# Seven blocks in the first group, deeper steps in the second, three raw slots instead of four

## The chip, the cores and the metric

One core of a Trainium2 chip runs the whole kernel. The metric is the device time of one execution in microseconds (us); the kernel before takes 721.62 us (median of three runs, 721.6 to 721.69). TensorE is called PE here, VectorE DVE, ScalarE ACT, GpSimd POOL and SyncE SP.

## The reference

`x` is 8192 x 128, `adj` is 8192 x 8192, W is 128 x 128, b has 128 values, all float32.

```python
h = maximum(layernorm(x), 0)
out = x + relu(adj @ (h @ W) + b)
```

The kernel computes `(adj @ h) @ W`. `adj` is 268 MB and has to be read once; that and the product adj @ h are nearly all of the work.

## The kernel before

**Tiling.** The 8192 rows of adj, which become output rows, are cut into 16 blocks of 512; the 8192 columns, over which is summed, into 64 k-tiles of 128. The product of one block and one k-tile is a [128 x 128] x [128 x 512] matmul into one of the eight PSUM banks; the tile of h is the weight and the piece of adj (transposed by the host, 256 KB) the moving side. Float32 precision comes from splitting: `high` is adj rounded to fp32r (ACT copies it, L404), `low` is the rest (DVE subtracts, L543), h has both halves too, and every block and k-tile gets three matmuls in a row of kinds: high x h_high, high x h_low, low x h_high (`product`, L582 to L587). The first two k-tiles of the first group (FOUR_PASS) aren't split: PE multiplies plain float32 (L627) while the vector engines are still at the layer norm.

**Groups and steps.** The blocks are worked in four groups of 6, 2, 6 and 2 (WIDTHS). A step t takes `DEPTHS` k-tiles of all blocks of its group: one k-tile in the wide groups, three in the narrow ones, so that every step has six blocks' worth of adj (1.5 MB). There are 64 + 22 + 64 + 22 = 172 steps, numbered through. A step's adj comes in pieces (`split_of`, L71): three pieces of two blocks in steps 2 to 23, two of three blocks in steps 24 to 63, and one piece of six in all later steps but the last. Each piece has its own DMA, and ACT, DVE and PE wait piece by piece (`parts_of`, L94; steps 4 to 9 halve their last piece block by block).

**Buffers.** `raw` has 4 slots (what DMA brings), `high` 3, `low` 2. SP issues the loads of step t once DVE has finished `low` of step t - 4 (L297). ACT writes high of step t after low of step t - 3 and PE's use of high of step t - 3 (L399, L400). DVE writes low of step t after all products of step t - 2 (L539). PE waits for the parts of high and of low (L642, L657).

**Layer norm.** During the first group x is loaded in 17 batches; DVE, ACT and POOL compute mean, variance and the normalised z, and ACT and DVE make h_high and h_low, four k-tiles at a time.

**Draining a group.** While a group runs, the blocks of the one before are drained in other PSUM banks. Step `FIRST_STEP + DRAIN_AT[c]` drains block c (`drained_at`, L160): there ACT copies the sum (L384) and DVE takes the rest (L498); one step later (PROJECT_AFTER) PE multiplies with W in three matmuls (`project`, L605); four steps later (FINISH_AFTER) DVE adds and takes the maximum (`finish`, L502); nine steps later (STORE_AFTER) SP stores. The residual x of the block, 256 KB, is loaded by SP in the draining step itself (`load_residual`, L273), into one of four slots of `x_sb`, after that slot's last store has landed (L278); POOL adds the bias to it (L356). SP does all that in one queue with the loads of adj: a wait for a store or for an output holds up the adj loads behind it. PE starts the third and fourth group only when all blocks of the group before the last are finished (L639). The last two blocks are closed one by one (L691 to L707).

Of the kernel before, what the change touches and what calls it, by code (L numbers as in the profile page):

```python
# [7 lines left out]
BANK = 512  # L8
N = 8192
TILES = N // P  # L10
COL_BLOCKS = N // BANK
# [1 line left out]

WIDTHS = [6, 2, 6, 2]
DEPTHS = [1, 3, 1, 3]
FIRST_BLOCK = [0, 6, 8, 14]
FIRST_BANK = [0, 6, 0, 6]
STEPS = [-(-TILES // d) for d in DEPTHS]  # L20
FIRST_STEP = [sum(STEPS[:g]) for g in range(len(WIDTHS))]
ALL_STEPS = sum(STEPS)
LAST = ALL_STEPS - 1

RAW_SLOTS, HIGH_SLOTS, LOW_SLOTS = 4, 3, 2
WIDEST = max(w * d for w, d in zip(WIDTHS, DEPTHS)) * BANK


# [5 lines left out]

FOUR_PASS = 2

NARROW_UNTIL = 24

HALVED_SINGLY = range(4, 10)

LOW_AT_ONCE_UNTIL = 7
WARMING, WARM = 2, 448
X_SLOTS = 4
Z_SLOTS = 2


DRAIN_AT = [3, 6, 8, 11, 13, 16]
PROJECT_AFTER, FINISH_AFTER, STORE_AFTER = 1, 4, 9
OUT_SLOTS = 2
EPS = 1e-5  # L50

# [19 lines left out]
def split_of(t):  # L71

    g = group_of(t)
    if t == 0:
        return [1, 1, 2, 2]
    if g == 0:
        return [3, 3] if t < FOUR_PASS or t >= NARROW_UNTIL else [2, 2, 2]
    return [1] * WIDTHS[g] if t == LAST else [WIDTHS[g]]


# [79 lines left out]
def drained_at(t, after):  # L160

    for g in range(len(WIDTHS) - 1):
        for c in range(WIDTHS[g]):
            if FIRST_STEP[g + 1] + DRAIN_AT[c] + after == t:
                return FIRST_BLOCK[g] + c
    return None

# [6 lines left out]
def gnn_layer(nc, x_batches, x_blocks, adj_piece, W, b, out_blocks):  # L174
    with ExitStack() as ctx:  # L175
# [36 lines left out]
        raw_landed = [[sem(f"raw_landed{s}_{i}") for i in range(4 if s == 0 else 3)] for s in range(RAW_SLOTS)]  # L212
        x_landed = [sem(f"x_landed{s}") for s in range(X_SLOTS)]
        x_first_landed = sem("x_first_landed")
        res_landed = [sem(f"res_landed{s}") for s in range(X_SLOTS)]
        params_landed = sem("params_landed")
        constants_ready = sem("constants_ready")
        warm_ready = sem("warm_ready")
# [27 lines left out]
        last_sum_ready = sem("last_sum_ready")  # L246
        last_projected = sem("last_projected")
        output_ready = sem("output_ready")
        stored = [sem(f"stored{s}") for s in range(X_SLOTS)]
        block = ctx.enter_context(nc.Block())  # L250

        def columns(t):
            g = group_of(t)
# [5 lines left out]
        @block.sync  # L259
        def _(sp):  # L260
            def load_x(j):

                if j == 5:
                    sp.wait_ge(centred, EARLY)
                if j > 5:
                    sp.wait_ge(z_ready, BATCHES[j - X_SLOTS][1] - EARLY)
                sp.dma_start(x_sb[:, x_slot(j), :], x_batches[j]).then_inc(x_landed[x_slot(j)], 16)  # L267

            def load_piece(t, i):
                sp.dma_start(raw[:, t % RAW_SLOTS, columns_of(t, blocks_of(t, i))], adj_piece(t, i)) \  # L270
                  .then_inc(raw_landed[t % RAW_SLOTS][i], 16)

            def load_residual(n):  # L273
                if n < X_SLOTS:

                    sp.wait_ge(z_ready, TILES - EARLY)
                else:
                    sp.wait_ge(stored[n % X_SLOTS], 16 * (n // X_SLOTS))  # L278
                sp.dma_start(x_sb[:, n % X_SLOTS, :], x_blocks[n]).then_inc(res_landed[n % X_SLOTS], 16)

            def store(n):
                sp.wait_ge(output_ready, n + 1)
                sp.dma_start(out_blocks[n], x_sb[:, n % X_SLOTS, :]).then_inc(stored[n % X_SLOTS], 16)

            sp.dma_start(x_sb[:, 0, 0:P], x_batches[0]).then_inc(x_first_landed, 16)  # L285

            for i in (0, 2, 3):
                load_piece(0, i)
            for t in range(1, ALL_STEPS):
                if t == 2:  # L290
                    load_x(3)
                if RAW_SLOTS <= t < RAW_SLOTS + FOUR_PASS:

                    sp.wait_ge(products_done, t - RAW_SLOTS + 1)
                if t >= RAW_SLOTS + FOUR_PASS:

                    sp.wait_ge(low_ready, halved(t - RAW_SLOTS))  # L297
                for i in range(len(split_of(t))):
                    load_piece(t, i)
                if mean_at(t) is not None:  # L300
                    load_x(mean_at(t))
                if t == 30:
                    sp.dma_start(W_sb[:, :], W).then_inc(params_landed, 16)
                    sp.dma_start(bias[:, :], b).then_inc(params_landed, 16)
                n = drained_at(t, 0)
                if n is not None:
                    load_residual(n)
                n = drained_at(t, STORE_AFTER)
                if n is not None:
                    store(n)  # L310
            for n in range(FIRST_BLOCK[-1], COL_BLOCKS):
                load_residual(n)
            for t in range(ALL_STEPS, ALL_STEPS + STORE_AFTER):
                n = drained_at(t, STORE_AFTER)
                if n is not None:
                    store(n)
            for n in range(FIRST_BLOCK[-1], COL_BLOCKS - 1):
                store(n)
            n = COL_BLOCKS - 1
            sp.wait_ge(output_ready, n + 1)  # L320
            sp.dma_start(out_blocks[n][:, 0:HALF], x_sb[:, n % X_SLOTS, 0:HALF]).then_inc(stored[n % X_SLOTS], 16)
            for s in range(X_SLOTS):

                sp.wait_ge(stored[s], 16 * (COL_BLOCKS // X_SLOTS + (s == n % X_SLOTS)))

        @block.gpsimd
        def _(pool):
            nc.gpsimd.memset(minus_half[:, :], -0.5).then_inc(constants_ready, 1)
            pool.wait_ge(constants_ready, 1)
            for j, (first, end) in enumerate(BATCHES):  # L330
                pool.wait_ge(var_ready, j + 1)
                nc.gpsimd.tensor_tensor(rstd[:, first:end], var_eps[:, first:end],  # L332
                                        minus_half[:, first:end], ALU.pow).then_inc(rstd_ready, 1)
                if j < 2:
                    continue
                pool.wait_ge(rstd_ready, j + 1)
                if j < SUMMED_BY_DVE:
                    pool.wait_ge(centre_ready, j + 1)

                if j == 3:  # L340
                    pool.wait_ge(h_first_ready, FOUR_PASS)
                    pool.wait_ge(early_low, EARLY - FOUR_PASS)
                if j > 3:
                    pool.wait_ge(h_low_ready, BATCHES[j - Z_SLOTS][1] - EARLY)
                for t in range(first, end):
                    cols = slice(t % 4 * P, t % 4 * P + P)
                    nc.gpsimd.tensor_scalar(z_sb[:, x_slot(j) % Z_SLOTS, cols],  # L347
                                            x_sb[:, x_slot(j), cols],
                                            neg_mean[:, t:t + 1], rstd[:, t:t + 1],
                                            ALU.add, ALU.mult).then_inc(z_ready, 1)  # L350
            pool.wait_ge(params_landed, 32)
            nc.gpsimd.tensor_scalar(neg_bias[:, :], bias[:, :], -1.0, None, ALU.mult).then_inc(neg_bias_ready, 1)
            for n in range(COL_BLOCKS):

                pool.wait_ge(res_landed[n % X_SLOTS], 16 * (n // X_SLOTS + 1))
                nc.gpsimd.tensor_scalar(x_sb[:, n % X_SLOTS, :], x_sb[:, n % X_SLOTS, :], bias[:, 0:1], None,  # L356
                                        ALU.add).then_inc(x_biased, 1)

        @block.scalar
        def _(act):  # L360
# [60 lines left out]
            for half in range(2):  # L421
# [1 line left out]
                nc.scalar.activation(last_sum[:, cols], banks[:, bank_of(n), cols],  # L423
                                     ACT.Copy).then_inc(last_sum_ready, 1)
            act.wait_ge(output_ready, n + 2)
            act.dma_start(out_blocks[n][:, HALF:BANK], x_sb[:, n % X_SLOTS, HALF:BANK]) \
               .then_inc(stored[n % X_SLOTS], 16)

        @block.vector
        def _(dve):  # L430
# [71 lines left out]
            def finish(n):  # L502
                dve.wait_ge(x_biased, n + 1)
                dve.wait_ge(projected, n + 1)
                nc.vector.scalar_tensor_tensor(x_sb[:, n % X_SLOTS, :], banks[:, bank_of(n), :], neg_bias[:, 0:1],  # L505
                                               x_sb[:, n % X_SLOTS, :], ALU.max, ALU.add) \
                  .then_inc(output_ready, 1)

            def finish_last(half):
                n = COL_BLOCKS - 1  # L510
                cols = slice(half * HALF, (half + 1) * HALF)
                dve.wait_ge(last_projected, half + 1)
                nc.vector.scalar_tensor_tensor(x_sb[:, n % X_SLOTS, cols], banks[:, half, 0:HALF],  # L513
                                               neg_bias[:, 0:1], x_sb[:, n % X_SLOTS, cols],
                                               ALU.max, ALU.add).then_inc(output_ready, 1)

            for cols in (slice(0, P), slice(P, WARM)):
# [63 lines left out]
        def _(pe):  # L581
# [49 lines left out]
            for t in range(FOUR_PASS, LAST - 1):  # L631
# [2 lines left out]
                opens, closes = s == 0, s == STEPS[g] - 1  # L634
                depths = range(depth_of(t))
                parts = parts_of(t)
                if opens and g >= 2:

                    pe.wait_ge(output_ready, FIRST_BLOCK[g - 1])  # L639

                def with_high(part):
                    pe.wait_ge(high_ready, halved(t, part))  # L642
                    if part == 0:
                        high_is_there(t)
                    for k in depths:
# [102 lines left out]
```

## Time and profile before

| what | value |
|---|---|
| median of three runs | 721.62 us |
| the profiled execution | 721.9 us |
| its span, first to last instruction | 720.1 us |
| PE busy, matmuls | 715.2 us (99%), 3113 |
| PE weight loads | 583.8 us (81%) |
| DVE busy | 623.3 us (87%) |
| ACT busy | 517.5 us (72%) |
| POOL busy | 181.4 us (25%) |
| DMA | 281.60 MB, mean 391 GB/s |
| granted PE clock | 1.00 throughout |

The profile is of one execution; 1.8 us of it lie outside the span, and it is 0.3 us above the median. Matmuls overlap in the pipeline: one is shown as 390 ns long though a new one starts about every 227 ns. So PE's idle time is read best from the idle time before its weight loads (PEld), which is 0.04 us where nothing is waited for. "Landing" is the time from the issue of a DMA to its completion.

### The profile page before, as it was taken

To read this page: it belongs to the slowest core of one execution; us is meant where nothing else is said; L and a number is where in the kernel's file an instruction comes from. 1 tells how busy PE (TensorE), PEld (TensorE's weight loads), DVE (VectorE), ACT (ScalarE), POOL (GpSimd) and SP (SyncE) were. 2 spreads that over 40 slices of the span, in tenths; PEclk is the share of its full clock that TensorE was granted. 3 is DMA by queue.
4 is the path that set the end of the run, shared out by engine and by line. 5 is a ranking of instruction groups with operands and counts; after the bars stand their busy time and mean duration, and the time that the engine had idled before them with its cause. 6 is when DMAs were issued, how large, how long until landed. Compare 5 with 4: busy or idle time off the path is not lost.

```text
span 720.1 us, 7905 instructions
## 1 busy us (share of the span) xinstructions
PE 715.2 (99%) x3113; PEld 583.8 (81%) x3113; DVE 623.3 (87%) x394; ACT 517.5 (72%) x400; POOL 181.4 (25%) x99
## 2 busy tenths in 40 slices
PE   9999999999999999999999999999999999999998
PEld 4878888888888888888888888888888888888886
DVE  5999999999999888988798888878788887888895
ACT  2788888888888767766577667667676676767662
POOL 4445555556544402410041000000000000033023
PEclk9999999999999999999999999999999999999999
DMA  9999999999999999999999999999999999999992
GB/s 353 408 408 409 409 411 415 412 415 416 417 415 414 418 421 407 415 387 404 359 410 428 383 402 396 364 397 386 379 390 391 382 391 385 398 403 397 389 382 77
DMA packets 45110, 281.60 MB, mean 391 GB/s; under 512 B 5137, under 2 KB 5777, under 8 KB 31505
## 3 DMA queue, kind: packets, MB, share of 16 engines
q1 hardware_dynamic: 44496, 280.25, 97.2%
q10 hardware_dynamic: 576, 0.85, 0.4%
q8 instruction: 24, 0.39, 0.2%
q14 instruction: 14, 0.11, 0.0%
HBM read 276.89 MB, written 4.19 MB: 390 GB/s over the span
## 4 chain that ended last, share of the span: by engine, by line
PE 94%; DMA 3%; DVE 1%; SPq 0%; ACT 0%; issue 0%; DVEq 0%; ACTq 0%
PE banks L585 93%; DMA raw<-adj 3%; DVE low L543 1%; PE banks L612 0%; PE banks L613 0%; PE banks L611 0%; SPq L270 0%; ACT high L404 0%; DVE h_low L489 0%; DVE x_sb L505 0%; DVE x_sb L513 0%; SPq L267 0%; DVEq L175 0%; SPq L285 0%; ACTq L403 0%
## 5 line engine op out<-in xcount | busy, mean ns | idle before, releaser
L543 DVE TENSOR_TENSOR low<-raw,high 128x3072 fp32r<-128x3072 f32 (+3 forms) x261 | 576.5, 2235 | 83.1 <-PE banks L585 69.9
L404 ACT ACTIVATE high<-raw 128x3072 fp32r<-128x3072 f32 (+3 forms) x261 | 483.6, 1864 | 188.6 <-DMA raw<-adj 160.7
L585 PE MATMUL banks<-high,h_high 128*128 128x512 f32 x1012 | 272.7, 390 | 0.1
L585 PE MATMUL banks<-high,h_low 128*128 128x512 f32 x1012 | 272.0, 389 | 0.0
L585 PE MATMUL banks<-low,h_high 128*128 128x512 f32 x1012 | 268.5, 389 | 0.0
L585 PEld LDWEIGHTS banks<-high,h_high 128*128 128x128 f32 x1012 | 189.6, 188 | 41.1 <-ACT high L404 1.6
L585 PEld LDWEIGHTS banks<-low,h_high 128*128 128x128 f32 x1012 | 189.7, 188 | 40.1 <-DVE low L543 0.8
L585 PEld LDWEIGHTS banks<-high,h_low 128*128 128x128 f32 x1012 | 190.0, 188 | 39.5
L356 POOL TENSOR_SCALAR x_sb<-x_sb,bias 128x512 f32<-128x512 f32 x16 | 54.5, 3409 | 414.2 <-DMA x_sb<-x_blocks 414.2
L347 POOL TENSOR_SCALAR z_sb<-x_sb,neg_mean,rstd 128x128 f32<-128x128 f32 x60 | 94.7, 1590 | 1.6
L332 POOL TENSOR_TENSOR rstd<-var_eps,minus_half 128x4 f32<-128x4 f32 (+2 forms) x17 | 31.6, 1860 | 112.8 <-DVE var_eps L447 103.6
L369 ACT ACTIVATE squares<-x_sb,neg_mean 128x128 f32<-128x128 f32 x52 | 20.1, 387 | 0.0
L384 ACT ACTIVATE sum_high<-banks 128x512 fp32r<-128x512 f32 x15 | 8.7, 580 | 7.0 <-PE banks L585 7.0
L505 DVE SCALAR_TENSOR_TENSOR x_sb<-banks,neg_bias,x_sb 128x512 f32<-128x512 f32 x15 | 11.2, 744 | 2.2 <-PE banks L613 2.2
L498 DVE TENSOR_TENSOR sum_low<-banks,sum_high 128x512 fp32r<-128x512 f32 x15 | 10.3, 683 | 2.1 <-ACT sum_high L384 2.1
L627 PE MATMUL banks<-raw,h_first 128*128 128x512 f32 x24 | 11.1, 607 | 0.2
L489 DVE SCALAR_TENSOR_TENSOR h_low<-z_sb,h_high 128x512 fp32r<-128x512 f32 x15 | 10.3, 690 | 0.0
L627 PEld LDWEIGHTS banks<-raw,h_first 128*128 128x128 f32 x24 | 4.2, 189 | 7.5 <-issue 4.5
L369 ACT ACTIVATION_READ_ACCUMULATOR squares<-x_sb,neg_mean 128x1 f32 x52 | 9.8, 188 | 0.0
L376 ACT ACTIVATE h_high<-z_sb 128x512 fp32r<-128x512 f32 x15 | 9.2, 614 | 0.0
L436 DVE TENSOR_REDUCE neg_sum<-x_sb 128x4 f32<-128x512 f32 x13 | 8.8, 674 | 0.0
L458 DVE BATCH_NORM_STATS2 stats<-x_sb 128x6 f32<-128x128 f32 x12 | 2.7, 282 | 4.4 <-DMA x_sb<-x 4.4
(34 smaller groups left out, 47.8 us busy)
## 6 DMA issues: line engine op xcount, KB each, us to landing
raw<-adj SPq DMA_DIRECT2D x106, 1536.0 KB, 8.6
raw<-adj SPq DMA_DIRECT2D x82, 768.0 KB, 10.6
raw<-adj SPq DMA_DIRECT2D x69, 512.0 KB, 11.9
x_sb<-x_blocks SPq DMA_DIRECT2D x16, 256.0 KB, 8.4
out_blocks<-x_sb SPq DMA_DIRECT2D x15, 256.0 KB, 8.7
x_sb<-x SPq DMA_DIRECT2D x14, 256.0 KB, 12.2
raw<-adj SPq DMA_DIRECT2D x3, 256.0 KB, 6.5
raw<-adj ACTq DMA_DIRECT2D x1, 256.0 KB, 2.8
```

The costliest lines, as they stand in the source:

```text
L332: nc.gpsimd.tensor_tensor(rstd[:, first:end], var_eps[:, first:end], minus_half[:, first:end], ALU.pow).then_inc(rstd_ready, 1)
L347: nc.gpsimd.tensor_scalar(z_sb[:, x_slot(j) % Z_SLOTS, cols], x_sb[:, x_slot(j), cols], neg_mean[:, t:t + 1], rstd[:, t:t + 1], ALU.add, A ...
L356: nc.gpsimd.tensor_scalar(x_sb[:, n % X_SLOTS, :], x_sb[:, n % X_SLOTS, :], bias[:, 0:1], None, ALU.add).then_inc(x_biased, 1)
L369: nc.scalar.activation(squares[:, before % 4, :], x_sb[:, x_slot(j), cols], ACT.Square, bias=neg_mean[:, t:t + 1], accum_out=sum_squares[: ...
L376: nc.scalar.activation(h_high[:, first:end, :], z_sb[:, x_slot(j) % Z_SLOTS, :].rearrange("p (t d) -> p t d", d=P), ACT.Relu).then_inc(h_h ...
L404: nc.scalar.activation(high[:, t % HIGH_SLOTS, cols], raw[:, t % RAW_SLOTS, cols], ACT.Copy).then_inc(high_ready, 1)
L489: nc.vector.scalar_tensor_tensor(h_low[:, first:end, :], z_sb[:, x_slot(j) % Z_SLOTS, :] .rearrange("p (t d) -> p t d", d=P), 0.0, h_high[ ...
L498: nc.vector.tensor_tensor(sum_low[:, n % OUT_SLOTS, :], banks[:, bank_of(n), :], sum_high[:, n % OUT_SLOTS, :].bitcast(F32), ALU.subtract) ...
L505: nc.vector.scalar_tensor_tensor(x_sb[:, n % X_SLOTS, :], banks[:, bank_of(n), :], neg_bias[:, 0:1], x_sb[:, n % X_SLOTS, :], ALU.max, ALU ...
L543: nc.vector.tensor_tensor(low[:, t % LOW_SLOTS, cols], raw[:, t % RAW_SLOTS, cols], high[:, t % HIGH_SLOTS, cols].bitcast(F32), ALU.subtra ...
L585: return nc.tensor.matmul(banks[:, FIRST_BANK[g] + c, :], h[:, (t - FIRST_STEP[g]) * DEPTHS[g] + k, :], tile[:, slot, at:at + BANK], start ...
L627: last = nc.tensor.matmul(banks[:, FIRST_BANK[0] + c, :], h_first[:, t, :], raw[:, t, c * BANK:(c + 1) * BANK], start=t == 0, stop=False)
```

## The change

The groups become 7, 1, 6 and 2 blocks wide, and the second takes six k-tiles a step, so it has 11 steps of 1.5 MB (the last of four k-tiles) and all together are 161. The first group's steps have seven blocks (1.75 MB). Buffers of a step are as wide as the widest step, so each slot grows from 6 to 7 blocks, and `raw` goes from 4 slots to 3; high and low keep 3 and 2. Pieces are [1, 1, 2, 3] in step 0, [4, 3] in step 1 and from step 20 to 63, [3, 2, 2] between; the third group's steps come in two pieces of three blocks instead of one of six. Draining: the six blocks of banks 0 to 5 are drained in steps 1, 2, 4, 5, 7 and 8 of the second group; the seventh stays in bank 6 and is drained in step 15 counted from the second group's start, which is step 4 of the third (counted from 0), and the second group's only block in step 8 of the third. The fourth group drains as before. Finishing comes three steps after draining (four before), storing eight (nine before), and the residual is loaded two steps ahead. Residuals have six slots: the four of `x_sb` and the two of `z_sb`. The opening step of the third and fourth group waits part by part for the banks that this part writes.

```diff
--- before.py
+++ after.py
@@ -13,16 +13,16 @@
 
 
 
-WIDTHS = [6, 2, 6, 2]
-DEPTHS = [1, 3, 1, 3]
-FIRST_BLOCK = [0, 6, 8, 14]
-FIRST_BANK = [0, 6, 0, 6]
+WIDTHS = [7, 1, 6, 2]
+DEPTHS = [1, 6, 1, 3]
+FIRST_BLOCK = [0, 7, 8, 14]
+FIRST_BANK = [0, 7, 0, 6]
 STEPS = [-(-TILES // d) for d in DEPTHS]
 FIRST_STEP = [sum(STEPS[:g]) for g in range(len(WIDTHS))]
 ALL_STEPS = sum(STEPS)
 LAST = ALL_STEPS - 1
 
-RAW_SLOTS, HIGH_SLOTS, LOW_SLOTS = 4, 3, 2
+RAW_SLOTS, HIGH_SLOTS, LOW_SLOTS = 3, 3, 2
 WIDEST = max(w * d for w, d in zip(WIDTHS, DEPTHS)) * BANK
 
 
@@ -34,18 +34,20 @@
 
 FOUR_PASS = 2
 
-NARROW_UNTIL = 24
+NARROW_UNTIL = 20
 
 HALVED_SINGLY = range(4, 10)
 
 LOW_AT_ONCE_UNTIL = 7
 WARMING, WARM = 2, 448
 X_SLOTS = 4
+RES_SLOTS = 6
 Z_SLOTS = 2
 
 
-DRAIN_AT = [3, 6, 8, 11, 13, 16]
-PROJECT_AFTER, FINISH_AFTER, STORE_AFTER = 1, 4, 9
+
+DRAIN_AT = [[1, 2, 4, 5, 7, 8, 15], [8], [3, 6, 8, 11, 13, 16]]
+RESIDUAL_AHEAD, PROJECT_AFTER, FINISH_AFTER, STORE_AFTER = 2, 1, 3, 8
 OUT_SLOTS = 2
 EPS = 1e-5
 
@@ -72,9 +74,11 @@
 
     g = group_of(t)
     if t == 0:
-        return [1, 1, 2, 2]
+        return [1, 1, 2, 3]
     if g == 0:
-        return [3, 3] if t < FOUR_PASS or t >= NARROW_UNTIL else [2, 2, 2]
+        return [4, 3] if t < FOUR_PASS or t >= NARROW_UNTIL else [3, 2, 2]
+    if g == 2:
+        return [3, 3]
     return [1] * WIDTHS[g] if t == LAST else [WIDTHS[g]]
 
 
@@ -161,7 +165,7 @@
 
     for g in range(len(WIDTHS) - 1):
         for c in range(WIDTHS[g]):
-            if FIRST_STEP[g + 1] + DRAIN_AT[c] + after == t:
+            if FIRST_STEP[g + 1] + DRAIN_AT[g][c] + after == t:
                 return FIRST_BLOCK[g] + c
     return None
 
@@ -212,7 +216,7 @@
         raw_landed = [[sem(f"raw_landed{s}_{i}") for i in range(4 if s == 0 else 3)] for s in range(RAW_SLOTS)]
         x_landed = [sem(f"x_landed{s}") for s in range(X_SLOTS)]
         x_first_landed = sem("x_first_landed")
-        res_landed = [sem(f"res_landed{s}") for s in range(X_SLOTS)]
+        res_landed = [sem(f"res_landed{s}") for s in range(RES_SLOTS)]
         params_landed = sem("params_landed")
         constants_ready = sem("constants_ready")
         warm_ready = sem("warm_ready")
@@ -246,8 +250,13 @@
         last_sum_ready = sem("last_sum_ready")
         last_projected = sem("last_projected")
         output_ready = sem("output_ready")
-        stored = [sem(f"stored{s}") for s in range(X_SLOTS)]
+        stored = [sem(f"stored{s}") for s in range(RES_SLOTS)]
         block = ctx.enter_context(nc.Block())
+
+        def residual(n):
+
+            slot = n % RES_SLOTS
+            return x_sb[:, slot, :] if slot < X_SLOTS else z_sb[:, slot - X_SLOTS, :]
 
         def columns(t):
             g = group_of(t)
@@ -274,13 +283,16 @@
                 if n < X_SLOTS:
 
                     sp.wait_ge(z_ready, TILES - EARLY)
+                elif n < RES_SLOTS:
+
+                    sp.wait_ge(h_low_ready, TILES - EARLY)
                 else:
-                    sp.wait_ge(stored[n % X_SLOTS], 16 * (n // X_SLOTS))
-                sp.dma_start(x_sb[:, n % X_SLOTS, :], x_blocks[n]).then_inc(res_landed[n % X_SLOTS], 16)
+                    sp.wait_ge(stored[n % RES_SLOTS], 16 * (n // RES_SLOTS))
+                sp.dma_start(residual(n), x_blocks[n]).then_inc(res_landed[n % RES_SLOTS], 16)
 
             def store(n):
                 sp.wait_ge(output_ready, n + 1)
-                sp.dma_start(out_blocks[n], x_sb[:, n % X_SLOTS, :]).then_inc(stored[n % X_SLOTS], 16)
+                sp.dma_start(out_blocks[n], residual(n)).then_inc(stored[n % RES_SLOTS], 16)
 
             sp.dma_start(x_sb[:, 0, 0:P], x_batches[0]).then_inc(x_first_landed, 16)
 
@@ -302,12 +314,12 @@
                 if t == 30:
                     sp.dma_start(W_sb[:, :], W).then_inc(params_landed, 16)
                     sp.dma_start(bias[:, :], b).then_inc(params_landed, 16)
-                n = drained_at(t, 0)
-                if n is not None:
-                    load_residual(n)
                 n = drained_at(t, STORE_AFTER)
                 if n is not None:
                     store(n)
+                n = drained_at(t, -RESIDUAL_AHEAD)
+                if n is not None:
+                    load_residual(n)
             for n in range(FIRST_BLOCK[-1], COL_BLOCKS):
                 load_residual(n)
             for t in range(ALL_STEPS, ALL_STEPS + STORE_AFTER):
@@ -318,10 +330,10 @@
                 store(n)
             n = COL_BLOCKS - 1
             sp.wait_ge(output_ready, n + 1)
-            sp.dma_start(out_blocks[n][:, 0:HALF], x_sb[:, n % X_SLOTS, 0:HALF]).then_inc(stored[n % X_SLOTS], 16)
-            for s in range(X_SLOTS):
-
-                sp.wait_ge(stored[s], 16 * (COL_BLOCKS // X_SLOTS + (s == n % X_SLOTS)))
+            sp.dma_start(out_blocks[n][:, 0:HALF], residual(n)[:, 0:HALF]).then_inc(stored[n % RES_SLOTS], 16)
+            for s in range(RES_SLOTS):
+
+                sp.wait_ge(stored[s], 16 * (len(range(s, COL_BLOCKS, RES_SLOTS)) + (s == n % RES_SLOTS)))
 
         @block.gpsimd
         def _(pool):
@@ -352,8 +364,8 @@
             nc.gpsimd.tensor_scalar(neg_bias[:, :], bias[:, :], -1.0, None, ALU.mult).then_inc(neg_bias_ready, 1)
             for n in range(COL_BLOCKS):
 
-                pool.wait_ge(res_landed[n % X_SLOTS], 16 * (n // X_SLOTS + 1))
-                nc.gpsimd.tensor_scalar(x_sb[:, n % X_SLOTS, :], x_sb[:, n % X_SLOTS, :], bias[:, 0:1], None,
+                pool.wait_ge(res_landed[n % RES_SLOTS], 16 * (n // RES_SLOTS + 1))
+                nc.gpsimd.tensor_scalar(residual(n), residual(n), bias[:, 0:1], None,
                                         ALU.add).then_inc(x_biased, 1)
 
         @block.scalar
@@ -423,8 +435,8 @@
                 nc.scalar.activation(last_sum[:, cols], banks[:, bank_of(n), cols],
                                      ACT.Copy).then_inc(last_sum_ready, 1)
             act.wait_ge(output_ready, n + 2)
-            act.dma_start(out_blocks[n][:, HALF:BANK], x_sb[:, n % X_SLOTS, HALF:BANK]) \
-               .then_inc(stored[n % X_SLOTS], 16)
+            act.dma_start(out_blocks[n][:, HALF:BANK], residual(n)[:, HALF:BANK]) \
+               .then_inc(stored[n % RES_SLOTS], 16)
 
         @block.vector
         def _(dve):
@@ -502,16 +514,16 @@
             def finish(n):
                 dve.wait_ge(x_biased, n + 1)
                 dve.wait_ge(projected, n + 1)
-                nc.vector.scalar_tensor_tensor(x_sb[:, n % X_SLOTS, :], banks[:, bank_of(n), :], neg_bias[:, 0:1],
-                                               x_sb[:, n % X_SLOTS, :], ALU.max, ALU.add) \
+                nc.vector.scalar_tensor_tensor(residual(n), banks[:, bank_of(n), :], neg_bias[:, 0:1],
+                                               residual(n), ALU.max, ALU.add) \
                   .then_inc(output_ready, 1)
 
             def finish_last(half):
                 n = COL_BLOCKS - 1
                 cols = slice(half * HALF, (half + 1) * HALF)
                 dve.wait_ge(last_projected, half + 1)
-                nc.vector.scalar_tensor_tensor(x_sb[:, n % X_SLOTS, cols], banks[:, half, 0:HALF],
-                                               neg_bias[:, 0:1], x_sb[:, n % X_SLOTS, cols],
+                nc.vector.scalar_tensor_tensor(residual(n)[:, cols], banks[:, half, 0:HALF],
+                                               neg_bias[:, 0:1], residual(n)[:, cols],
                                                ALU.max, ALU.add).then_inc(output_ready, 1)
 
             for cols in (slice(0, P), slice(P, WARM)):
@@ -634,12 +646,12 @@
                 opens, closes = s == 0, s == STEPS[g] - 1
                 depths = range(depth_of(t))
                 parts = parts_of(t)
-                if opens and g >= 2:
-
-                    pe.wait_ge(output_ready, FIRST_BLOCK[g - 1])
 
                 def with_high(part):
                     pe.wait_ge(high_ready, halved(t, part))
+                    if opens and g >= 2:
+
+                        pe.wait_ge(output_ready, FIRST_BANK[g] + parts[part][1][-1] + 1)
                     if part == 0:
                         high_is_there(t)
                     for k in depths:
```

## Rows read from the trace of the kernel before

**Rows 1.** The page: busy share, then the granted clock in 40 slices.

```profile
PE 715.2 (99%) x3113; PEld 583.8 (81%) x3113; DVE 623.3 (87%) x394; ACT 517.5 (72%) x400; POOL 181.4 (25%) x99
...
PEclk9999999999999999999999999999999999999999
```

**Rows 2.** Busy time by stretch: PE, PEld, DVE, ACT, POOL, clock, DMA share, GB/s.

```profile
352.00:614.00 262.00, 262.00 (x1157) 216.91 (x1156) 217.91 (x70) 177.63 (x66) 10.60 (x2) 1.00 0.99 392
614.00:705.00 91.00, 91.00 (x402) 75.19 (x401) 78.64 (x33) 62.99 (x30) 21.87 (x7) 1.00 0.98 388
sum 645.00, PE 645.00 PEld 533.71 DVE 566.03 ACT 475.17 POOL 152.19; mean PE 129.00 PEld 106.74 DVE 113.21 ACT 95.03 POOL 30.44
```

**Rows 3.** Waits from 60 to 712 us: us in total, times, longest.

```profile
ACT high L404 <- DMA raw<-adj: 143.4, 142, 3.0
...
DVE low L543 <- PE banks L585: 69.9, 89, 2.9
```

**Rows 4.** Waits in the first 60 us.

```profile
PEld banks L627 <- DMA raw<-adj: 1.7, 2, 1.0
PEld banks L585 <- ACT high L404: 1.6, 5, 0.5
...
PEld banks L585 <- DVE low L543: 0.8, 3, 0.4
```

**Rows 5.** PE's weight loads at the start: start us, us, in brackets idle before.

```profile
8.68 0.30 PEld L627 LDWEIGHTS banks<-raw,h_first 128*128 128x128 f32 x2 [0.95 <-DMA raw<-adj]
9.22 0.19 PEld L627 LDWEIGHTS banks<-raw,h_first 128*128 128x128 f32 x1 [0.24 <-issue]
...
15.34 0.19 PEld L585 LDWEIGHTS banks<-high,h_high 128*128 128x128 f32 x1 [0.29 <-ACT high L404]
...
36.79 0.30 PEld L585 LDWEIGHTS banks<-high,h_high 128*128 128x128 f32 x2 [0.48 <-ACT high L404]
```

**Rows 6.** Busy time by stretch at the start, columns as in rows 2.

```profile
4.00:15.30 11.30, 11.06 (x25) 4.23 (x24) 6.55 (x37) 1.06 (x1) 4.61 (x8) 1.00 1.03 412
15.30:60.00 44.70, 44.61 (x193) 35.33 (x192) 41.70 (x47) 37.94 (x57) 18.29 (x10) 1.00 1.03 408
```

**Rows 7.** Groups by shape, whole span: busy us, mean ns, idle before.

```profile
L543 DVE TENSOR_TENSOR low<-raw,high 128x3072 fp32r<-128x3072 f32 x106 | 356.2, 3363 | 69.4 <-PE banks L585 63.8 <-ACT high L404 4.2
L404 ACT ACTIVATE high<-raw 128x3072 fp32r<-128x3072 f32 x106 | 294.6, 2779 | 139.5 <-DMA raw<-adj 115.7 <-PE banks L585 14.4 <-DVE low L543 9.3
...
L543 DVE TENSOR_TENSOR low<-raw,high 128x1536 fp32r<-128x1536 f32 x80 | 139.3, 1771 | 8.8 <-PE banks L585 6.1 <-ACT high L404 2.2
L404 ACT ACTIVATE high<-raw 128x1536 fp32r<-128x1536 f32 x80 | 118.1, 1486 | 23.6 <-DMA raw<-adj 23.4
...
L543 DVE TENSOR_TENSOR low<-raw,high 128x1024 fp32r<-128x1024 f32 x61 | 72.3, 1235 | 4.0 <-ACT high L404 3.5
```

**Rows 8.** SP's own waits, whole span.

```profile
SPq L270 <- DVE low L543: 544.9, 162, 4.8
SPq L279 <- DMA out_blocks<-x_sb: 23.4, 5, 4.8
```

**Rows 9.** One step of the third group, in order of time.

```profile
468.78 2.78 ACT L404 ACTIVATE high<-raw 128x3072 fp32r<-128x3072 f32 x1 [1.27 <-DMA raw<-adj]
...
472.32 0.33 SPq L270 DMA_DIRECT2D raw<-adj  x1
...
472.59 1.32 PEld L585 LDWEIGHTS banks<-high,h_high 128*128 128x128 f32 x6
...
473.01 3.36 DVE L543 TENSOR_TENSOR low<-raw,high 128x3072 fp32r<-128x3072 f32 x1 [0.72 <-PE banks L585]
```

**Rows 10.** Landing of adj loads: from 355 us (one load), 440 to 560, 600 to 697.

```profile
DMA to landing us min/median/max: 6.9/6.9/6.9
...
DMA to landing us min/median/max: 7.3/8.4/10.2
...
DMA to landing us min/median/max: 6.5/8.9/11.1
```

## The prediction

> **What bounds the kernel now.** I read the page first: PE is busy 99% of the span, at the full granted clock in all 40 slices [rows 1]. Busy matmul time alone can hide gaps, so the next view is busy time by stretch: from 60 to 705 us PE has no idle time at all (645.00 of 645.00 us), and the 1157 matmuls of 352 to 614 us take 262 us, 0.2267 us each [rows 2]. A step of 18 matmuls is thus 4.08 us. The waits say the same: from 60 us on, ACT waits for DMA (143 us) and DVE for PE (70 us), and no row has PE waiting for anything [rows 3]. These waits are slack of engines that run ahead. PE waits only in the first 60 us: 1.6 us for high, 0.8 us for low, and before that for two pieces of adj [rows 4]. Of the 2.4 us some 0.04 us in each of eight waits is the ordinary spacing, so about 2.1 us could be won there; everything else of PE is its count of matmuls. So the change can gain very little, and the question is what it can lose.
>
> **PE's work.** The order of groups doesn't change the number of products, except that the two unsplit k-tiles now cover seven blocks. An unsplit product is two matmul records, each 0.43 us from weight load to weight load (0.19 busy, 0.24 idle) [rows 5], so 0.86 us; a split one is three of 0.2267, 0.68 us. Two products change kind: 2 x (0.86 - 0.68) = +0.35 us. The projections stay 15 x 3 matmuls.
>
> **The start.** PE stood still until the last piece of step 0 had landed, 0.95 us before the load at 8.68 [rows 5]. That piece now has three blocks instead of two. DMA moves 412 GB/s here [rows 6], so 256 KB more (262144 bytes) come 0.64 us later: +0.64 us, whole, since PE already waited for this piece. Then the balance turns. Step 2 began on PE as its first part became ready (0.29 us idle, on ACT, at 15.34) [rows 5]. Now adj for it comes three blocks later (one in each of steps 0 and 1, one in the first part): 1.9 us, and ACT takes 1.49 us for three blocks [rows 7] instead of 1.06 for two [rows 6], 2.4 us in all; PE comes to it 0.64 + 2 x 0.86 = 2.4 us later. It stays in balance. After that each step gives more room than before: 21 matmuls are 4.76 us against 7.25 blocks of DMA (a quarter for x) x 0.64 = 4.64, so DMA gains 0.12 us a step; before it was 4.08 against 6.25 x 0.64 = 4.00, 0.08 us. DVE has 1.77 + 2 x 1.24 = 4.25 us of subtractions [rows 7] for 4.76, before 3 x 1.24 = 3.71 for 4.08: with 0.4 us of other work a step it goes from 101% to 98%. I credit 0.35 of the 2.1 us of early waits, those on low and part of the wait at 36.79 [rows 5]; bounds 0 and 1.2, as the waits on DMA remain. Sum so far: 0.35 + 0.64 - 0.35 = +0.64 us.
>
> **SP's queue.** Five residual loads waited 23.4 us in all for stores, with adj loads queued behind them [rows 8]. With six slots and loads two steps ahead no wait is left: the store of block n goes out four or more steps before the load of block n + 6. This is worth 0, since PE never waited in that stretch; the cover is the lead of the raw slots. The loads and stores are the same in number. They are denser: six residuals in eight steps of the second group make 8 x 3.7 + 6 x 0.64 = 33.4 us of DMA against 8 x 4.08 + 5 projections x 0.68 = 36.0 us of PE. They fit.
>
> **Draining sooner.** ACT copies block 0 at step 1 of the group, and for that has to wait until PE closes the first group. High of that step is done some 2.7 us sooner, so ACT loses 2.7 us, with the loads of high queued behind it; high is ready 4 us before PE wants it, so 0. DVE's finish of block 5 falls in the opening step of the third group and gates that step's second part: two halves 3.5 us and the finish 0.74 from the close of the step before last put it 0.3 to 1.0 us ahead of PE. 0 again, but the margin is thin. The seventh block in bank 6 and block 7 in bank 7 are finished some 55 steps before the fourth group writes them. The tail keeps its order: 0.
>
> **Three raw slots.** This is the term I can't read off. In a step of the third group before, high is written at 468.78 as its piece lands, done at 471.56, and DVE subtracts at 473.01 when PE frees the low slot [rows 9]: DMA is 1.45 us early. PE would notice only when low is late by a further 3.4 us (DVE starts a step ahead, takes 3.36 us of 4.08, and low is wanted 2.72 us into the step). So there are 4.85 us in hand. A slot less issues each load 4.08 us later; 0.77 us are left if a load still takes the 8.4 us it took at the median [rows 10]. Where the stage has single pieces it must also hold as a loop: low done, load, ACT 2.78, DVE 3.36 [rows 7] and 0.1 of signals make 6.24 us plus landing, against three steps of PE, 12.24 us, and 0.56 more for the projections of the fourth group. Landing may take 6.6 us. The shortest full load took 6.9, in a thin queue; the median of 440 to 560 us is 8.4, of 600 to 697 us 8.9 [rows 10]. Bounds for the fourth group's seven loops: at 6.9 us, 0.34 x 7 = 2.4 us of lateness, under the 3.4 us in hand: 0. At 8.9 us, 2.34 x 7 = 16.4, less 3.4: +13 us. But landing includes time behind the loads issued before, and a load issued later stands behind less, so I take it near 6.9, with +0.3 us for single late loads. In the third group half pieces shorten the loop to 1.49 + 1.77 + 0.1 [rows 7], which leaves 8.9 us for landing: 0. The second group has six projections in 11 steps and allows 7.1 us. A rule of the Trainium skill (DMA: Bandwidth & Descriptors, "Anatomy of one DMA") has about 2.0 us fixed and the bytes at 436 GB/s: estimated 5.6 us for 1.57 MB, with which the loop would hold with 1.0 us to spare. The trace shows more than that even in the shortest load [rows 10].
>
> **Sum.** +0.64 + 0.3 = +0.9 us on the profiled 721.9, 722.8; on the median, which is 0.3 us lower, 721.6 + 0.9 = 722.5.
>
> **Rivals.** No change for a measurement of this kernel means within 0.2%, 1.44 us: 720.2 to 723.1.
> (A) The forecast, PE's count and the start decide: 722.5, own range 721.4 to 723.1. Chance 0.52.
> (B) The three slots starve PE. Place: the fourth group above all, then the second, and the thin gate at the third group's opening. It decides when landing in the single-piece stages stays over about 7.1 us, where seven loops of 0.5 us eat the 3.4. At 7.5 us: 0.9 x 7 = 6.3, less 3.4 = +2.9 us, on 722.3: about 725; at 7.9 us 728. For it: the median landings, ACT's 142 waits for DMA [rows 3], DMA busy 98% in these stretches [rows 2], landings of 10 and 11 us. Against it: before, the queue was always filled a step further ahead, and DMA idles more when issued later. Chance 0.43. The Trainium skill (DMA: Bandwidth & Descriptors, "Latency and other measured facts") puts HBM access at 0.2 us on average and 2 us under high load, and has it dominate the fixed cost, which speaks for this case; no row here separates access from queueing.
> (C) The early waits vanish wholly and the larger piece is partly hidden: 721.6 + 0.35 - 2.1 + 0.3 = 720.2, at the edge. Chance 0.05, of which 0.03 beyond the edge.
> Faster 0.03, same 0.52, slower 0.45 (B and a little of a worse start). The range leaves out 0.1 on either side: 721.4 to 727.
>
> **What would show it.** Right: PE's first weight load of L585 near 18.0 us, 14 unsplit products, no wait of PE from 60 us on up to the second group, SP without waits on stores. Rival B: PE weight loads waiting for DVE low or ACT high at steps of 4.08 us in the last 95 us, landing above 7 us there and SP issuing on low late. Wrong altogether would be a different spacing of matmuls from 0.2267 us, or a wait at the opening of the third group above 1 us.

## The result, and the profile after

The changed kernel takes 737.87 us (median of six runs, 734.95 to 741.53) against 721.66 us: ratio 1.0228, 95% interval 1.02 to 1.0255. It is 16.2 us slower. The prediction was 722.5 us with a range up to 727 us; the time lies 11 us outside. What happened is rival B, at 16 us where the prediction priced it at 2.9 us (landing 7.5 us) and 5.7 us (7.9 us). The profiled execution took 738.19 us, its span is 736.4 us.

The page of the changed kernel: span, busy time, and in 40 slices PE's busy tenths and the bandwidth (to hold against [rows 1]).

```profile
span 736.4 us, 8028 instructions
...
PE 722.7 (98%) x3111; PEld 582.3 (79%) x3111; DVE 626.4 (85%) x443; ACT 525.3 (71%) x449; POOL 171.6 (23%) x99
...
PE   9999999999999999999999999999999999989897
...
GB/s 358 411 411 411 412 418 418 416 414 418 410 404 402 400 393 381 402 359 329 339 421 371 419 412 413 384 387 373 397 367 409 381 391 388 335 335 366 361 350 130
```

PE's missing tenths are at the end, and bandwidth falls there and in slices 18 to 20. Busy time by stretch, with the columns of [rows 2]:

```profile
60.00:300.00 240.00, 240.00 (x1060) 198.72 (x1060) 221.90 (x163) 196.09 (x223) 109.27 (x61) 1.00 1.01 407
...
345.00:400.00 55.00, 53.75 (x230) 42.12 (x229) 48.19 (x30) 36.53 (x26) 3.90 (x2) 1.00 0.98 376
400.00:560.00 160.00, 160.00 (x707) 132.48 (x706) 138.73 (x82) 118.71 (x80) 0.00 (x0) 1.00 0.99 393
...
635.00:725.00 90.00, 83.86 (x351) 64.26 (x350) 69.40 (x31) 53.94 (x27) 10.45 (x6) 1.00 0.92 342
```

The counts in brackets tell more than busy time. At 0.2267 us a matmul, 55 us hold 243 and had 230: 2.9 us lost around the second group's end. 90 us hold 397 and had 351: 10.4 us lost in the fourth group. From 60 to 300 us and from 400 to 635 us nothing is lost; from 300 to 345 us there are 198 matmuls, where a run below without waits has 200, and the last 11 us lose a little more. A few records can be missing from a trace, so these counts are good to about 1 us. The waits from 60 to 712 us name the cause, where [rows 3] had none for PE:

```profile
PEld banks L597 <- DVE low L555: 10.3, 16, 0.9
PEld banks L597 <- ACT high L416: 6.2, 8, 2.0
```

L597 is the line of the split matmuls and of their weight loads; L555 writes low and L416 writes high in the changed kernel. One stretch of the fourth group in order of time shows the chain:

```profile
682.15 2.77 ACT L416 ACTIVATE high<-raw 128x3072 fp32r<-128x3072 f32 x1 [1.79 <-DMA raw<-adj]
...
684.98 1.23 PEld L597 LDWEIGHTS banks<-high,h_high 128*128 128x128 f32 x6 [0.34 <-ACT high L416]
685.03 3.36 DVE L555 TENSOR_TENSOR low<-raw,high 128x3072 fp32r<-128x3072 f32 x1 [0.42 <-ACT high L416]
...
688.41 0.33 SPq L279 DMA_DIRECT2D raw<-adj  x1
688.44 1.22 PEld L597 LDWEIGHTS banks<-low,h_high 128*128 128x128 f32 x6 [0.87 <-DVE low L555]
```

ACT waits for the load, DVE starts 0.1 us after ACT ends, PE waits for DVE, and at 688.41, 0.02 us after low is done, SP issues the load of three steps later. Every link waits for the one before it: this is the loop of the prediction, running closed. The landings of the fourth group's loads (642 to 713 us) are at the median 8.5 us, against 8.9 us before [rows 10] and 9.2 us for the kernel before's loads of 635 to 691 us alone. They are shorter by 0.4 to 0.7 us, not by the 2 us that the prediction counted on:

```profile
L279 SPq DMA_DIRECT2D raw<-adj x15: 327/328/328, 642.5 to 712.9; - x15
...
DMA to landing us min/median/max: 6.5/8.5/9.9
```

15 issues in 70.4 us are 5.03 us a step, against 4.27 that PE needs there with its projections.

At the start the steps came as worked out. The rows answer to [rows 5]; L639 is the line of the unsplit matmuls:

```profile
9.30 0.30 PEld L639 LDWEIGHTS banks<-raw,h_first 128*128 128x128 f32 x2 [0.61 <-DMA raw<-adj]
...
17.74 0.67 PEld L597 LDWEIGHTS banks<-high,h_high 128*128 128x128 f32 x3 [0.42 <-ACT high L416]
19.54 0.53 PEld L597 LDWEIGHTS banks<-low,h_high 128*128 128x128 f32 x3 [0.44 <-DVE low L555]
```

### The profile page after: what moved, and what is told of

It is laid out like the page before. It is cut to its first block, busy times and chain, and to the rows that moved or that the text cites. A ratio compares the mean times of both kernels' runs of the same rounds, so it can differ in the third digit from the quotient of the medians.

```text
span 736.4 us, 8028 instructions
## 1 busy us (share of the span) xinstructions
PE 722.7 (98%) x3111; PEld 582.3 (79%) x3111; DVE 626.4 (85%) x443; ACT 525.3 (71%) x449; POOL 171.6 (23%) x99
## 4 chain that ended last, share of the span: by engine, by line
PE 76%; DMA 12%; DVE 6%; ACT 4%; issue 1%; DVEq 0%; ACTq 0%
PE banks L597 73%; DMA raw<-adj 12%; DVE low L555 6%; ACT high L416 4%; PE banks L639 2%; PE banks L631 0%; DVE x_sb L517 0%; PE banks L625 0%; PE banks L624 0%; PE banks L623 0%; DVE sum_low L510 0%; DVE last_sum L530 0%; DVE x_sb L525 0%; ACTq L415 0%; DVEq L179 0%
## 5 line engine op out<-in xcount | busy, mean ns | idle before, releaser
L555 DVE TENSOR_TENSOR low<-raw,high 128x1536 fp32r<-128x1536 f32 (+4 forms) x310 | 579.7, 1902 | 96.1 <-ACT high L416 67.6
L416 ACT ACTIVATE high<-raw 128x1536 fp32r<-128x1536 f32 (+4 forms) x310 | 489.6, 1598 | 199.5 <-DMA raw<-adj 180.7
L597 PE MATMUL banks<-low,h_high 128*128 128x512 f32 x1010 | 278.9, 391 | 5.7 <-DVE low L555 5.7
L597 PE MATMUL banks<-high,h_high 128*128 128x512 f32 x1010 | 281.0, 391 | 3.3 <-ACT high L416 3.2
L597 PE MATMUL banks<-high,h_low 128*128 128x512 f32 x1010 | 279.5, 389 | 0.0
L597 PEld LDWEIGHTS banks<-low,h_high 128*128 128x128 f32 x1010 | 188.0, 188 | 51.7 <-DVE low L555 13.3
L597 PEld LDWEIGHTS banks<-high,h_high 128*128 128x128 f32 x1010 | 188.9, 188 | 46.2 <-ACT high L416 6.9
L597 PEld LDWEIGHTS banks<-high,h_low 128*128 128x128 f32 x1010 | 189.6, 188 | 39.6
L368 POOL TENSOR_SCALAR x_sb<-x_sb,bias 128x512 f32<-128x512 f32 x12 | 29.2, 2434 | 382.0 <-DMA x_sb<-x_blocks 382.0
L359 POOL TENSOR_SCALAR z_sb<-x_sb,neg_mean,rstd 128x128 f32<-128x128 f32 x60 | 104.2, 1748 | 1.6
L344 POOL TENSOR_TENSOR rstd<-var_eps,minus_half 128x4 f32<-128x4 f32 (+2 forms) x17 | 27.7, 1630 | 145.6 <-DVE var_eps L459 135.0
L368 POOL TENSOR_SCALAR z_sb<-z_sb,bias 128x512 f32<-128x512 f32 x4 | 10.0, 2492 | 29.1 <-DMA z_sb<-x_blocks 29.1
L639 PE MATMUL banks<-raw,h_first 128*128 128x512 f32 x28 | 13.5, 641 | 0.0
L639 PEld LDWEIGHTS banks<-raw,h_first 128*128 128x128 f32 x28 | 5.6, 209 | 8.3 <-issue 6.4
L501 DVE SCALAR_TENSOR_TENSOR h_low<-z_sb,h_high 128x512 fp32r<-128x512 f32 x15 | 10.4, 690 | 0.0
L517 DVE SCALAR_TENSOR_TENSOR x_sb<-banks,neg_bias,x_sb 128x512 f32<-128x512 f32 x11 | 8.2, 743 | 2.2 <-PE banks L625 2.2
```

Of the source, the lines that this page charges most:

```text
L368: nc.gpsimd.tensor_scalar(residual(n), residual(n), bias[:, 0:1], None, ALU.add).then_inc(x_biased, 1)
L416: nc.scalar.activation(high[:, t % HIGH_SLOTS, cols], raw[:, t % RAW_SLOTS, cols], ACT.Copy).then_inc(high_ready, 1)
L501: nc.vector.scalar_tensor_tensor(h_low[:, first:end, :], z_sb[:, x_slot(j) % Z_SLOTS, :] .rearrange("p (t d) -> p t d", d=P), 0.0, h_high[ ...
L555: nc.vector.tensor_tensor(low[:, t % LOW_SLOTS, cols], raw[:, t % RAW_SLOTS, cols], high[:, t % HIGH_SLOTS, cols].bitcast(F32), ALU.subtra ...
L597: return nc.tensor.matmul(banks[:, FIRST_BANK[g] + c, :], h[:, (t - FIRST_STEP[g]) * DEPTHS[g] + k, :], tile[:, slot, at:at + BANK], start ...
L639: last = nc.tensor.matmul(banks[:, FIRST_BANK[0] + c, :], h_first[:, t, :], raw[:, t, c * BANK:(c + 1) * BANK], start=t == 0, stop=False)
```

## The experiments

Theory 1: with three raw slots, a step that comes in one piece can't be loaded, split and freed within three steps of PE. Theory 2: the shape of the groups, above all the dense draining, costs it.

**Three slots in the kernel before.**

```diff
-RAW_SLOTS, HIGH_SLOTS, LOW_SLOTS = 4, 3, 2
+RAW_SLOTS, HIGH_SLOTS, LOW_SLOTS = 3, 3, 2
```

> The kernel before with three raw slots instead of four and nothing else changed. Theory 1 (a slot less starves PE where a step comes in one piece): here every step from 64 on is one piece, the third group too, so it loses at least what the changed kernel lost, 10 to 30 us over 721.7. Theory 2 (the loss comes from the shape of the groups, the dense draining of seven blocks in eleven steps, and the slots don't matter): 721.7, within 1 us.

803.75 us (four runs, 799.78 to 807.81), ratio 1.1127 (1.1075 to 1.1179): 82 us slower by one number alone. The theory holds, and my 10 to 30 us were far too low: of the 108 steps from 64 on, all but the last are one piece here. From 500 to 600 us, SP's loads:

```profile
L270 SPq DMA_DIRECT2D raw<-adj x21: 327/328/328, 501.0 to 599.3; - x21
...
DMA to landing us min/median/max: 6.8/8.4/9.1
```

98.3 us for 20 intervals are 4.92 us a step. The loop gives (8.4 + 6.24)/3 = 4.88. So the loop's form was right, and landing is 8.4 us, the median that the four-slot kernel has from 440 to 560 us [rows 10].

**Four slots back, for the later groups.** In the changed kernel, raw as one memory of 24 blocks (48 KB a partition instead of 42; the squares, the first h and the warm-up tile live in its unused end during the first group).

```diff
+def raw_columns(t, cols):
+    if t < FIRST_STEP[1]:
+        start = (t % RAW_SLOTS) * WIDTHS[0] * BANK
+    else:
+        start = (LATER_SLOTS - 1 - (t - FIRST_STEP[1]) % LATER_SLOTS) * 6 * BANK
+    return slice(start + cols.start, start + cols.stop)
...
-                    sp.wait_ge(low_ready, halved(t - RAW_SLOTS))
+                    sp.wait_ge(low_ready, halved(free_after(t)))
```

`free_after` is t - 3 in the first group, t - 4 from step 68, and steps 62, 62, 63, 63 for the four between.

> The changed kernel with raw as 24 blocks of memory: three slots of seven blocks in the first group, four slots of six in the others. Theory 1: the waits of PE after 300 us go, 721.5 to 723. Theory 2: stays at 733 to 740. If the second group's stall comes from its draining and the fourth's from the slots, some 4 us stay: 726.

723.07 us, ratio 1.0012 (1.0003 to 1.0022). 14.8 of the 16.2 us are gone, with the groups' shape and the dense draining kept. Theory 2 falls. The time lies 0.07 us above the range I gave; PE's weight loads still wait 1.0 us for low, three times, around the second group.

**Only the new residual handling, on the kernel before** (groups, slots and draining steps as before; six residual slots, loads two steps ahead, finish after three steps, store after eight, gates by part).

```diff
-DRAIN_AT = [3, 6, 8, 11, 13, 16]
-PROJECT_AFTER, FINISH_AFTER, STORE_AFTER = 1, 4, 9
+DRAIN_AT = [[3, 6, 8, 11, 13, 16]] * 3
+RESIDUAL_AHEAD, PROJECT_AFTER, FINISH_AFTER, STORE_AFTER = 2, 1, 3, 8
```

> The kernel before (groups 6, 2, 6, 2, four slots) with only the new residual handling: six residual slots, loads two steps ahead, finish after three steps, store after eight, opening steps gated part by part. Both theories: 721.7 within 0.5 us, as no wait of PE hangs on it; SP's 23 us of waits for stores gone. A third theory (the denser queue of residuals and stores delays adj loads) would have it 1 us or more slower.

721.98 us, ratio 0.9999 (0.9989 to 1.0008). SP's own waits no longer have the line of [rows 8] with 23.4 us for stores. Beside those of the adj loads, the largest is that of two late stores for their output (L293 on DVE's L515, 17.9 us, at 705.26 and 717.1), behind all adj loads. So that part is worth nothing, as forecast.

**The fourth group in two pieces**, three slots kept.

```diff
-    return [1] * WIDTHS[g] if t == LAST else [WIDTHS[g]]
+    return [1] * WIDTHS[g]
```

> The changed kernel, three slots, with the fourth group's steps in two pieces of one block (three k-tiles) each. Theory 1 with the length of the loop as the cause: ACT 1.49 and DVE 1.77 in place of 2.78 and 3.36 shorten the loop by 2.9 us, so the fourth group's stalls (some 11 us) go nearly all: 725 to 729. If halves only help little because landing itself grows, 732 to 737. Theory 2 (draining): unchanged, 735 to 740.

727.16 us (four runs, 726.63 to 727.71), ratio 1.0067 (1.0052 to 1.0082): 10.7 us back.

**The same slots, each load issued as two.** On the kernel before with three slots, every one-piece load of 1.5 MB goes out as two DMAs of 768 KB; ACT waits for both.

```diff
+                    for k in range(2):
+                        sp.dma_start(raw[:, t % RAW_SLOTS, cols.start + k * half:cols.start + (k + 1) * half],
+                                     adj_piece(t, i)[:, k * half:(k + 1) * half]) \
+                          .then_inc(raw_landed[t % RAW_SLOTS][i], 16)
```

> The kernel before with three raw slots (803.75 us in that form), and each 1.5 MB load of steps 64 to 170 issued as two of 768 KB, whose rows are 6 KB instead of 12 KB; ACT still waits for both. If landing stays at 8.4 us because single long rows straggle (packets of 12 KB took up to 2.5 us against 0.46 at the median), it falls below 7.5 us and the time to 760 to 780. If it is the transfer and what it queues behind, nothing changes: 798 to 810.

801.21 us (four runs, 794.48 to 810.52), ratio 1.1063 (1.101 to 1.1116). That is 2.5 us under the run with whole loads, and the two intervals overlap, so no gain is clear of the noise. In the profiled execution (the slowest of the four) the 20 pairs of 500 to 600 us take, from the issue of the first half to the landing of the second, 8.4 us at the median: landing didn't fall either. The idea of straggling long rows is out as a way to win the time back; it is pieces for the engines that help, not smaller DMAs.

**Two slots.**

```diff
-RAW_SLOTS, HIGH_SLOTS, LOW_SLOTS = 4, 3, 2
+RAW_SLOTS, HIGH_SLOTS, LOW_SLOTS = 2, 3, 2
```

> The kernel before with two raw slots: at most one other load lies before a load. The loop is (landing + 6.24)/2 us a step in the 108 steps from 64 on. If landing shrinks as the queue gets thin, as the prediction had it, to 6.5 us: 6.4 us a step, 250 us more there, and some more in the first group. If it stays at 8.4 us: 7.3 us a step, 350 us more. Landing itself is read from the trace.

1052.52 us (one run). From 500 to 600 us:

```profile
L270 SPq DMA_DIRECT2D raw<-adj x15: 327/328/328, 503.4 to 595.8; - x15
...
DMA to landing us min/median/max: 6.1/6.4/9.1
```

Here landing does shrink, to 6.4 us. The loop gives (6.4 + 6.24)/2 = 6.3 us a step and the issues 92.4/14 = 6.6. So an adj load with almost nothing before it takes 6.4 us, but with three slots it still takes 8.4, as with four. Of the 331 us over the kernel before, some 88 us lie ahead of the first one-piece step: ACT comes to it at 352.36 instead of 263.94. The rest is near the 250 us expected there.

**Three slots, all later steps in pieces**, on the kernel before.

```diff
-    return [1] * WIDTHS[g] if t == LAST else [WIDTHS[g]]
+    return [3, 3] if g == 2 else [1] * WIDTHS[g]
```

> The kernel before with three raw slots and every step from 64 on in pieces: two of three blocks in the third group, two of one block (three k-tiles) in the second and fourth. The loop is 1.49 + 1.77 + 0.2 plus landing; with 8.0 us of landing 11.5 us against the 12.24 of three steps of PE. So nearly all of the 82 us goes: 722 to 727. If instead three slots cost through DMA throughput (idle gaps in the queue) and not through the loop, it stays above 750.

724.81 us (ten runs, 722.59 to 727.28), ratio 1.0036 (1.0022 to 1.005). 79 of the 82 us are gone at three slots. Had DMA throughput been the cause, this couldn't be. What is left shows in the trace as 3.3 us in which PE's weight loads wait for low.

**Better slots, pieces and start together**: the 24-block raw with its slots laid so that steps 64 to 67 wait for steps 61, 62, 63 and 63; the fourth group in pieces; step 0 in five pieces.

```diff
-        return [1, 1, 2, 3]
+        return [1, 1, 2, 1, 2]
...
-    return t % RAW_SLOTS if t < FIRST_STEP[1] else RAW_SLOTS + (t - FIRST_STEP[1]) % LATER_SLOTS
+    return (t + 1) % RAW_SLOTS if t < FIRST_STEP[1] else RAW_SLOTS + (t - FIRST_STEP[1]) % LATER_SLOTS
```

> The changed kernel with four later raw slots laid so that steps 64 to 67 wait for steps 61, 62, 63 and 63 (before: 62, 62, 63, 63), the fourth group in two pieces, and step 0 in pieces of 1, 1, 2, 1 and 2 blocks instead of 1, 1, 2 and 3. Against 723.07: the second group's waits for low (1.0 us) go, and PE's wait of 0.6 to 0.9 us for step 0's last piece shrinks to 0.1: 721.5, a hair under the kernel before or equal to it. If the start is bound by DMA all the same, 722.3.

722.28 us, ratio 1.0006 (0.9997 to 1.0015): the same as the kernel before, and not the 721.5 us I hoped for. PE has no wait left from 60 us on, so it is the start that the smaller pieces don't win.

**The second group in pieces as well**, three slots: its one block's six k-tiles are loaded, halved and multiplied three by three.

```diff
+    if g == 1:
+        return [depth_of(t) // 2] * 2
...
+                pairs = [[(0, k) for k in blocks] if g == 1 else
+                         [(c, k) for k in range(depth_of(t)) for c in blocks] for _, blocks in parts]
```

> The changed kernel with three slots and its dense draining, but with the second group's steps in two pieces of three k-tiles too, on top of the fourth group's (727.16 us with that alone). If the second group's waits (about 4 us) come from the length of the loop, they go: 722.5 to 724. If they come from draining six blocks in eight steps or from the gate at the third group's opening, 726.5 to 727.5.

722.20 us, ratio 1.0009 (0.9999 to 1.0018), 0.3 us under the range I gave. With 727.16 us for the fourth group's pieces alone, the second group's single pieces cost 5.0 us, and the dense draining and the gate at the third group's opening cost nothing by themselves. The same stretches as above, in this kernel:

```profile
345.00:400.00 55.00, 55.00 (x244) 45.48 (x243) 48.82 (x34) 38.53 (x29) 3.91 (x2) 1.00 1.00 391
...
635.00:700.00 65.00, 65.00 (x287) 53.69 (x286) 58.90 (x42) 47.35 (x37) 19.29 (x5) 1.00 1.01 401
```

PE is full again. From 60 to 712 us it waits for nothing; the waits are back with the engines that run ahead, DVE's for PE (46.2 us) and ACT's for DMA:

```profile
ACT high L419 <- DMA raw<-adj: 142.8, 209, 2.4
```

**Slots freed piece by piece**, on top.

```diff
+                    if t >= RAW_SLOTS + FOUR_PASS and by_piece:
+                        sp.wait_ge(low_ready, halved(t - RAW_SLOTS, i))
```

> The same, and SP waits for the low of one piece three steps back instead of the whole step, so that the first piece of a step is issued some 1.8 us sooner. Loop theory: what is left of waits after 60 us goes, 722.0 to 722.8 (0.35 us of unsplit products and 0.4 of the start over the kernel before). If it is DMA throughput that is left, no change against the run above.

722.15 us, ratio 1.0007 (0.9997 to 1.0017): no change, since nothing was left to win after 60 us. The run therefore doesn't tell the two readings that I had set against each other apart.

## Why the prediction was wrong, step by step

- **PE's floor**: right. Every version without starvation (the residual run, four later slots, and the last three) lies at 721.98 to 723.07 us, and none beat the kernel before. The row's own quotient, 262/1157, is 0.2264 us a matmul; the 0.2267 us used is 4.08/18, and 4.08 us is also the spacing of SP's issues in the third group before.
- **Unsplit products and the start**: right in the parts. The larger piece came at 9.30 instead of 8.68, 0.62 us later (forecast 0.64), and PE's first load of L597 was at 17.74 (forecast near 18.0). The sum of +0.64 us answers to 722.20 - 721.68 = 0.5 us in the run with all groups in pieces.
- **SP's queue, draining sooner, the thin gate**: right at 0, shown by the residual run and by the run with the second group in pieces. The waits of 23.4 us were hidden, and their end brings nothing. One figure of the working was off: six blocks at its own 0.64 us are 3.84 us of DMA a step, not 3.7, and the eight steps come to 34.6 us. That still fits in 36.0.
- **Three raw slots**: this step failed, and in one term. The loop and its 6.24 us beside landing were right, and the 3.4 us in hand fit, though no run measures them by themselves. But I took landing "near 6.9", and so the whole term at +0.3 us, because a load issued later would stand behind less. Landing was 8.5 us in the fourth group. With 8.5 the working reads (8.5 + 6.24)/3 = 4.91 us a step against 4.27, 0.64 x 22 = 14.2, less 3.4 in hand: 10.8 us, and the fourth group's pieces brought back 10.7.
- **The second group** failed by the same term: the prediction had a limit of 7.1 us for landing there but no cost. Its full steps take PE 4.45 us on average with the projections, and landing was 8.3 us at the median (300 to 345 us): 4.85 a step, 0.4 x 11 = 4.4 us. Less was in hand there: low of its first step was done at 314.16 and PE wanted it at 315.95, 1.8 us. On the other side, the loop also has DVE's work of draining in it: at 334.38 low starts 0.96 us after high is ready, behind such work. Its pieces brought back 5.0, so this sum fits only roughly. Both groups' pieces together are 15.7 of the 16.2 us; the six runs of the changed kernel spread over 6.6 us and the counts of its trace divide the loss otherwise, so the total is surer than the two parts.
- **The rule of the Trainium skill**: estimated 5.6 us by the Trainium skill (DMA: Bandwidth & Descriptors, "Anatomy of one DMA — SWDGE (gpsimd) path") against 6.4 us measured with two slots. The page gives its rule for DMAs that GpSimd issues, while SP issues these, which the prediction didn't say. Here it is 0.8 us short even for a load with little before it, and it says nothing of one in a full loop.
- **The range**: it left out a bound that the text itself had worked out, +13 us at the median landing of the last 100 us. A row that was the shortest of over 100 full loads (the 6.5 us in [rows 10] are a 256 KB piece's) was no basis for the middle of 22 steps. Nor was it a load with nothing before it: issued at 355.29, it had two full loads issued since the short one at 342.3, and the last of them had 2.7 us to go.
- **Open**: why landing stays at 8.4 us with three slots while it is 6.4 us with two. With three, a load is issued 4.9 us after the last, which then still has 3.5 us to go, so it does stand behind something; but evenly spaced loads of 4.2 us each (an estimate, 1.57 MB at the 372 GB/s of the last section) needn't queue. Nor does landing follow what is left of the last load: those issued at 516.5, 579.9 and 594.7 us with 2.0 to 2.4 us left took 8.4 to 8.5 us, the one at 546.0 with 2.4 left took 6.8. Whether uneven issues or the slowest of the 16 engines do it, no run here separates.

## What to carry to other kernels

Before a buffer slot is given up, add up the loop that the slot closes (landing as it stands under load, at the median, plus every engine's time from landing to release) and hold it against that many steps of the bounding engine. A piece shortens this loop, because ACT and DVE then handle half a step after the last landing instead of a whole one: three slots in halves nearly did what four whole ones did, while smaller DMAs alone did nothing that shows. That holds as long as landing itself doesn't change, so take it from a trace of the loaded queue. Here the waits on a queue that ran ahead were worth nothing when removed, but the lead that hid them was worth all it hid: one slot was 82 us.

## What the runs showed of the hardware that I had not expected

In these runs DMA moved fewer bytes per busy time the fewer slots there were. From 460 to 520 us, in the kernel before, with three slots and with two (columns of [rows 2]; the last two are the DMA share and GB/s):

```profile
460.00:520.00 60.00, 60.00 (x267) 49.67 (x266) 49.18 (x16) 40.78 (x15) 0.00 (x0) 1.00 0.98 383
```

```profile
460.00:520.00 60.00, 54.52 (x225) 41.08 (x225) 42.20 (x13) 34.83 (x14) 0.00 (x0) 1.00 0.88 327
```

```profile
460.00:520.00 60.00, 42.13 (x160) 30.25 (x159) 31.19 (x14) 24.79 (x11) 1.57 (x1) 0.94 0.69 243
```

383/0.98, 327/0.88 and 243/0.69 are 391, 372 and 352 GB/s of busy engines: 5% and 10% less. That may be part of why a landing doesn't shrink by all that it no longer waits; no run separates it. And in the last of these PE's granted clock averages 0.94 of the 2.4 GHz level. From 493.8 to 500.6 us it was granted the 1.2 GHz level, around a pause of 7.04 us in PE's weight loads that ended at 495.73. The next two groups of six weight loads took 2.21 and 2.46 us, later ones 1.32 us. After the shorter waits of the same stretch, 0.85 to 2.57 us, the clock stayed at 2.4 GHz. A long pause of PE can thus cost a little beyond the wait itself; how much of the time of this kernel, these runs don't separate.
